# GpSimd issues the first six pieces of the MLP weight ring ahead of two rstd computations, right behind its last update of x in the first attention stage

## What is computed

```python
x = x + tanh(g_xattn[0]) * _L0_xattn_ref(_layernorm(x), ctx_1024, ...)
x = x + tanh(g_ffn[0])   * _L0_ffn_ref(_layernorm(x), Wr, Wi, Wo)
x = x + tanh(g_xattn[1]) * _L1_xattn_ref(_layernorm(x), ctx_1024, mask, W, b)
x = x + tanh(g_ffn[1])   * _L1_ffn_ref(_layernorm(x), w1_w, w1_s, w2_w, w2_s, h1_w, h1_s, h2_w, h2_s, w3_w, w3_s)

def _L1_ffn_ref(x, ...):
    h = silu(_tlin(x, w1_w, w1_s)) * _tlin(x, w2_w, w2_s)
    h = gelu(_tlin(h, h1_w, h1_s)); h = gelu(_tlin(h, h2_w, h2_s))
    return _tlin(h, w3_w, w3_s)
```

## Time and profile before

| | |
|---|---|
| median of 3 runs | 1044.86 us (1043.34 to 1047.59) |
| the profiled execution, its own time | 1045.72 us |
| its span, first to last instruction | 1043.9 us |
| mean granted TensorE clock | 0.993 |
| busy: TensorE, VectorE, ScalarE, GpSimd | 97%, 49%, 46%, 29% |
| DMA | 158.85 MB, mean 152 GB/s |

### The profile page before, as it was taken

How to read it: one execution, slowest core, us unless ns; L and a number is a source line. 1 busy time by engine, 2 the same in 40 slices (tenths; PEclk the granted TensorE clock), 3 DMA queues, 4 the chain that set the end, 5 groups by cost and what they waited for, 6 DMA issues and landing times.

```text
span 1043.9 us, 14469 instructions
## 1 busy us (share of the span) xinstructions
PE 1009.0 (97%) x5250; PEld 830.6 (80%) x5250; DVE 511.7 (49%) x1407; ACT 477.0 (46%) x877; POOL 304.3 (29%) x428
## 2 busy tenths in 40 slices
PE   7999999989999999999999999999999999999996
PEld 4778777668789887877898878878888788788885
DVE  5487767866432553464325534653245355134321
ACT  1355544446544445365444453554444535434431
POOL 0015653401530542315304422144044222112111
PEclk9999999999999999999999999999999999999999
DMA  9930015423385455353754653437546535345440
GB/s 341 376 123 1 2 61 159 128 100 102 121 279 181 144 189 157 98 159 116 265 178 155 190 160 101 144 125 257 195 150 189 163 105 170 113 136 147 141 141 23
DMA packets 44252, 158.85 MB, mean 152 GB/s; under 512 B 6443, under 2 KB 6827, under 8 KB 43282
## 3 DMA queue, kind: packets, MB, share of 16 engines
q0 software_dynamic: 29952, 104.88, 32.7%
q1 hardware_dynamic: 10826, 40.63, 11.5%
q10 hardware_dynamic: 3400, 12.38, 3.0%
HBM read 137.93 MB, written 29.36 MB: 160 GB/s over the span
## 4 chain that ended last, share of the span: by engine, by line
PE 83%; DVE 8%; ACT 4%; issue 2%; DMA 1%; POOL 1%; SPq 0%; DVEq 0%; POOLq 0%; ACTq 0%
PE psum L1052 56%; PE psum L842 2%; PE psum L946 2%; PE psum L1124 2%; PE psum L1126 2%; PE psum L1125 2%; PE psum L1100 1%; PE psum L852 1%; PE psum L700 1%; PE psum L972 1%; PE psum L724 1%; PE psum L738 1%; PE psum L954 1%; DVE x_residual L1907 1%; PE psum L754 1%
## 5 line engine op out<-in xcount | busy, mean ns | idle before, releaser
L2301 POOL DMA_DIRECT2D mlp_pieces<-in_mlp x176 | 96.7, 559 | 415.1 <-PE psum L1052 411.6
L1052 PE MATMUL psum<-hidden_b_high,mlp_pieces 128*128 128x512 f32 x512 | 202.9, 396 | 0.0
L1052 PE MATMUL psum<-hidden_a_high,mlp_pieces 128*128 128x512 f32 x512 | 202.8, 396 | 0.0
L1052 PE MATMUL psum<-hidden_b_low,mlp_pieces 128*128 128x512 f32 x512 | 199.6, 390 | 0.0
L1052 PE MATMUL psum<-hidden_a_low,mlp_pieces 128*128 128x512 f32 x512 | 199.6, 390 | 0.0
L2146 DVE TENSOR_TENSOR hidden_a_low<-hidden_a,hidden_a_high 128x512 fp32r<-128x512 f32 x128 | 88.0, 688 | 174.2 <-ACT hidden_a_high L1522 173.4
L2146 DVE TENSOR_TENSOR hidden_b_low<-hidden_b,hidden_b_high 128x512 fp32r<-128x512 f32 x64 | 44.3, 693 | 157.0 <-ACT hidden_b_high L1522 157.0
L1539 ACT ACTIVATE hidden_a<-psum,mlp_scales 128x512 f32<-128x512 f32 x64 | 44.1, 689 | 154.5 <-PE psum L1052 154.4
L1052 PEld LDWEIGHTS psum<-hidden_a_high,mlp_pieces 128*128 128x128 f32 x512 | 96.1, 188 | 22.1 <-DVE hidden_a_low L2146 1.7
L1052 PEld LDWEIGHTS psum<-hidden_a_low,mlp_pieces 128*128 128x128 f32 x512 | 96.2, 188 | 20.3 <-issue 1.0
L1052 PEld LDWEIGHTS psum<-hidden_b_high,mlp_pieces 128*128 128x128 f32 x512 | 96.2, 188 | 20.1 <-issue 0.8
(11 more groups left out here) (291 smaller groups left out, 1840.2 us busy)
## 6 DMA issues: line engine op xcount, KB each, us to landing
mlp_pieces<-in_mlp POOLq DMA_DIRECT2D x176, 512.0 KB, 4.1
slots<-in_zeros SPq DMA_DIRECT2D x3, 3072.0 KB, 36.3
yrows<-expert_rows ACTq DMA_DIRECT2D x18, 512.0 KB, 3.2
mlp_piece_to_examine<-in_mlp SPq DMA_DIRECT2D x16, 512.0 KB, 4.1
slot_rows<-slots SPq DMA_DIRECT2D x15, 512.0 KB, 5.0
x_residual<-in_x SPq DMA_DIRECT2D x4, 1024.0 KB, 23.2
out<-x_residual SPq DMA_DIRECT2D x8, 512.0 KB, 3.4
expert_in<-in_Wi SPq DMA_DIRECT2D x1, 2048.0 KB, 16.0
```

The costliest lines, as they stand in the source:

```text
L1052: last = mm(o, a, b, start=(k == 0 and i == 0), stop=(k == n_k - 1 and i == len(parts) - 1))
L2301: pool.dma_start(mlp_ring[:, r % RING, :], d["mlp"][r % NCHECK]).then_inc(ring_in[r % RING], 16)
```

## The change

GpSimd's six `load_piece` move ahead of both `invert`, and get one more wait, on `xupd` for all 32 updates of x (its own last instruction before them). Nothing is added or removed otherwise.

```diff
@@ -2283,8 +2283,6 @@
                 if b < B - 2:
                     invert(b * JT + G, G, 2 * b + 2)
 
-            invert(0, G, STATS_A)
-            invert((B - 1) * JT + G, G, STATS_A + 1)
             def piece_free(r):
 
                 n, piece = r // NCHECK, r % NCHECK
@@ -2302,8 +2300,11 @@
 
             pool.wait_ge(fin, NT)
             pool.wait_ge(th_r, NT)
+            pool.wait_ge(xupd, NT)
             for r in range(RING):
                 load_piece(r)
+            invert(0, G, STATS_A)
+            invert((B - 1) * JT + G, G, STATS_A + 1)
             invert(0, G, 1, stats_c, inv_c)
             invert(G, G, STATS_A + 2)
 
```

## The result

| | before | after |
|---|---|---|
| median | 1044.91 us (5 runs, 1043.34 to 1047.59) | 1039.12 us (5 runs, 1038.46 to 1041.90) |
| profiled execution, span | 1043.9 us | 1037.3 us |

The ratio is 0.9943, 95% interval 0.9922 to 0.9965: 5.8 us less, where 5.0 were forecast. The change is faster beyond the noise, and by a little over the half per cent that was the bound; but the interval, 3.7 to 8.2 us, reaches across that bound of 5.2. Two more comparisons of the same kernel gave 0.9942 (0.9926 to 0.9957) and 0.9944 (0.9925 to 0.9963).

What follows compares the result with a forecast made beforehand. TensorE bounds the kernel, with 83% of the last-ending chain; time saved ahead of stage d is saved at the end. Stall 4.20 + clock 1.6 - late rstd 0.75 = 5.0 us, so 1044.86 - 5.0 = 1039.9 us, range 1037.4 to 1042.7.

Steps and rivals of the forecast that it cites:

- the half per cent that was the bound: About 0.5%, here 5.2 us: what a measurement of this kernel can tell from no change.
- The stall: TensorE's 4.20 us wait ahead of L960, ended by ScalarE's scores_c_T behind late ring pieces; forecast to go whole.
- The added wait: GpSimd's wait on xupd for its own last update of x, ahead of the issues; costed at nothing, at most 0.1 us.
- The issues: GpSimd's six ring-piece DMA issues, now ahead of both invert; forecast to take 3.42 us, from about 192.85 to 196.25.
- the rule that spoke against the change: Skill's shared-port rule: GpSimd issues blocked by VectorE take 3.1 us, six 18.6, making the kernel about 10 us slower.
- The late rstd: invert of group 0 now follows the issues, so VectorE's c_norm starts 0.75 us late, charged in full.
- The clock: Twelve TensorE matmuls soon after the stall, 4.42 us mostly at 1.2 GHz, would take 2.8 at full clock: 1.6 saved.
- The sum: Stall 4.20 plus clock 1.6 minus late rstd 0.75: stage d begins 5.0 us earlier, giving 1039.9 us.
- The clock rival: TensorE's clock falls at the longer gap ahead of c_turn, costing 1.6 us: gain 3.4, 1041.5 us; chance 0.09.
- The larger gain: Whole kernel gains over 5.2 us, from cheaper issues, quicker examinations or more slow matmuls in other executions; chance 0.40.
- The slower rival: Issues hold GpSimd, so rstd and c_norm; break-even at a 5.8 us delay, over 1.4 us per issue; chance 0.05.

Runs made afterwards that it cites:

- ScalarE's order alone: Kernel before, with only ScalarE's order changed: scores_c_T and probs_c ahead of examining ring pieces, GpSimd as before; 1042.74 us, ratio 0.9960.
- two pieces first: Changed kernel with two pieces issued ahead of invert of group 0, four behind it, then the other invert; run twice, medians 1037.84 and 1039.24 us.

## Why the prediction was right, and where not

- **The stall (4.20 us).** Right: it went whole, and nothing took its place at L960. The run with ScalarE's order alone shows the mechanism: it has no stall with the pieces as late as before. ScalarE's step came in time, 206.58 for a TensorE that reached L960 at 207.72.
- **The added wait, "I cost it at nothing, with 0.1 us as the other end".** This step failed. It costs 0.66 to 0.67 us in all seven profiles in which GpSimd's issue waits for its own last instruction, and the run with that wait added behind the rstd shows that it is the wait. The argument "it would finish before a later instruction anyway" took the instruction's end for the time at which the wait ends: without a wait the issue follows at once, with it 0.66 us later.
- **The issues (3.42 us).** Right to the hundredth: 3.42 in all three profiles of the changed kernel. The prediction took the rule that spoke against the change as a price of 3.1 us for each issue; what the runs bear out is a bound on when an issue ends. The Trainium skill ("SBUF — State Buffer", on the bandwidth-pool intuition) lets a blocked issue end about 115 ns behind VectorE's fast copy, and the rows show 0.11 and 0.13 us behind a cast. The 3.1 us that it names for an issue never came up: these casts last 0.4 us, and the longest issue beside one took 0.99 (in the two profiles with two pieces first). No cast runs beside the issues in the changed kernel.
- **The late rstd (-0.75 us).** Mis-sized by the 0.66 us of the wait: 1.43. That it is paid in full was right (1.43 of `c_norm`, 1.44 of the local interval).
- **The clock (1.6 us).** Right for the profile at hand, 4.71 against 3.09 from L960 to L966. In the second profile of the kernel before it was 2.5.
- **The sum.** 4.20 + 1.6 - 1.43 = 4.4, and 38.96 - 34.45 = 4.5 was measured. With the second profile of before, 39.95 - 34.45 = 5.5. Two errors of opposite sign, a dear wait and a clock that costs more in other executions, left the forecast of 5.0 near the middle; that it came so close is in part luck. The median's 5.8 lies above both. Its interval of 3.7 to 8.2 holds them, and the comparison of medians also holds the first stage's clock; that this makes the difference is likely, but not shown.
- **The clock rival.** It came true in one profile of three, and its price was mis-sized: 0.5 us instead of 1.6, for the reason above. In the run with VectorE's casts moved, a gap of 1.98 us ahead of `c_turn` left the clock up.
- **The larger gain,** at 0.40, is what the median shows, by 0.6 us over the bound, and its interval reaches across. The slower rival was not seen; its place was right (the issues do hold the rstd), its price was not reached.

How far the clock moves whole runs can be read from the runs with their mean granted clock. Of the kernel before, 12 runs at 0.992 have a mean span of 1045.1 us, five at 0.996 or 0.997 of 1041.1. Of the changed one, seven at 0.994 have 1039.8 and seven at 0.997 have 1037.0. At the like clock (0.996 to 0.997) the difference is 4.1 us; between the mean spans of all runs it is 1043.9 - 1038.2 = 5.7 (29 and 16 runs). A like mean clock is not a like first stage, since the kernel before has the slow stretch behind its stall in its mean and the changed one had such a stretch in one profile of three. So part of the change's gain is that one cause of slow stretches, the 4.2 us stall, is gone. That the first stage's variation is all the clock was read from the profiles and not tested by a run of its own.

## What to carry to other kernels

An engine that issues DMAs in program order delays them by every wait ahead of them: find the instruction whose wait is long (here one `invert` of two) and move the issues past that one alone. Moving them past short work that another engine hangs on gives part of the gain back, here 1.43 us of 5.9 (38.96 - 33.06). The other handle is the place of the buffer's reader: where it stands ahead of steps that don't need the buffer, they wait for a late piece too, and moving it behind them gave 2.85 us here with the pieces as late as before. Both together were not run.

## What the runs showed that was not expected

- A wait of GpSimd for its own last instruction ahead of a DMA issue costs 0.66 us; ahead of a TENSOR_TENSOR on the same engine (L2261 to L2262) 0.08.
- A cast on VectorE holds a GpSimd issue to 0.11 to 0.13 us behind its own end, so its price is between nothing and a little over its own duration (0.45 us for a cast of 0.41), by how the two fall.
- The stretch at TensorE's lower clock level behind the same 4.2 us stall cost 1.6 us in one execution and 2.5 in another; after a gap of 1.7 us the clock fell in one profile of three.
